# A two-layer graph network on one Trainium2 core: x W0 of the first layer by feature instead of by node

## The reference

```python
def first(x, adj, weight, bias):                 # layer 0
    y = einsum('nm,bmd->bnd', adj, x)
    return einsum('bnd,do->bno', y, weight) + bias

def gru(x, adj, ...):                            # layer 1, 3 steps, in_mat = out_mat = adj
    h = x
    for _ in range(3):
        a = einsum('nm,bmd->bnd', adj, h); av = concatenate([a, a])
        z = sigmoid(lin(av, w3, b3) + lin(h, u3, bu3))
        r = sigmoid(lin(av, w4, b4) + lin(h, u3, bu3))
        hv = tanh(lin(av, w5, b5) + lin(r * h, u5, bu5))
        h = (1 - z) * h + z * hv
    return h

x = layernorm(x + first(x, adj, W0, b0))
x = layernorm(x + gru(x, adj, ...))
```

## Time and profile before

| | us |
|---|---|
| median of 3 runs | 1602.19 (1601.06 to 1602.37) |
| the profiled execution, its time | 1599.25 |
| its span, first to last instruction | 1597.4 |
| TensorE busy | 1583.3 (99%) |
| VectorE busy | 1391.9 (87%) |
| ScalarE busy | 1153.9 (72%) |
| GpSimd busy | 336.0 (21%) |
| DMA | 297.50 MB, mean 186 GB/s |

### The profile page before, as it was taken

One profiled execution on the slowest core, in us unless ns is written; L12 is line 12 of the kernel. 1 busy time (PEld: TensorE's weight loads), 2 busy tenths in 40 slices (PEclk: granted clock), 3 DMA queues, 4 the chain that ended last, 5 costly groups with the idle time before them and its releaser, 6 DMA issues.

```text
span 1597.4 us, 21866 instructions
## 1 busy us (share of the span) xinstructions
PE 1583.3 (99%) x7402; PEld 1327.2 (83%) x7402; DVE 1391.9 (87%) x1416; ACT 1153.9 (72%) x2306; POOL 336.0 (21%) x392
## 2 busy tenths in 40 slices
PE   9999999999999999999999999999999999999996
PEld 8888888888888888888888888888888888888885
DVE  6988888889888898988989898898888898878887
ACT  5677677777777778777777677776777877776666
POOL 5111112123121221212221212212132121110013
PEclk9999999999999999999999999999999999999998
DMA  6555545766467754666646675466755566456544
GB/s 193 173 178 182 191 143 183 222 208 199 144 197 213 222 193 125 202 219 211 198 143 192 222 233 160 161 196 216 219 172 165 188 217 209 141 149 197 170 147 158
DMA packets 215617, 297.50 MB, mean 186 GB/s; under 512 B 21201, under 2 KB 183890, under 8 KB 215506
## 3 DMA queue, kind: packets, MB, share of 16 engines
q1 hardware_dynamic: 215088, 295.79, 59.3%
q10 hardware_dynamic: 418, 0.33, 0.1%
HBM read 149.76 MB, written 146.28 MB: 185 GB/s over the span
## 4 chain that ended last, share of the span: by engine, by line
PE 97%; SPq 1%; ACT 1%; DMA 1%; issue 0%; POOL 0%; DVE 0%; POOLq 0%; ACTq 0%
PE ps_r L462 48%; PE ps_h L462 32%; PE ps_a L562 8%; PE ps_l L519 5%; PE ps_l L529 2%; SPq L321 1%; PE ps_a L543 0%; DMA h_scratch_a<-h_blocks_a 0%; PE ps_a L631 0%; PE ps_l L486 0%; PE ps_h L486 0%; PE ps_l L506 0%; PE ps_h L506 0%; PE ps_a L506 0%; DMA h_landed_a<-h_scratch_a 0%
## 5 line engine op out<-in xcount | busy, mean ns | idle before, releaser
L1068 DVE STREAM_TRANSPOSE a_blocks<-ps_a 128x1024 f32<-128x1024 f32 x92 | 114.8, 1247 | 93.8 <-PE ps_a L562 93.6
L842 ACT ACTIVATE rh<-ps_r,bias_r 128x512 f32<-128x512 f32 x192 | 128.3, 683 | 82.8 <-PE ps_r L462 77.7
L678 ACT ACTIVATE rh_hi<-rh 128x512 fp32r<-128x512 f32 x192 | 119.0, 632 | 75.6 <-DVE rh L1096 75.4
L854 ACT ACTIVATE z_sb<-ps_r,bias_z 128x512 f32<-128x512 f32 x192 | 126.5, 681 | 39.1 <-PE ps_r L462 38.3
L1108 DVE TENSOR_TENSOR hv<-hv,z_sb 128x1024 f32<-128x1024 f32 x95 | 127.6, 1343 | 10.3 <-DVE hv L1105 0.5
L947 DVE TENSOR_TENSOR rh_lo<-rh,rh_hi 128x512 fp32r<-128x512 f32 x192 | 125.7, 688 | 9.2
L858 ACT ACTIVATE hv<-ps_h,bias_h 128x512 f32<-128x512 f32 x192 | 121.0, 676 | 11.9 <-PE ps_h L462 11.9
L462 PE MATMUL ps_r<-a_hi_a,w_hi 128*128 128x512 f32 x384 | 118.8, 391 | 0.5 <-ACT rh L842 0.5
L462 PE MATMUL ps_h<-rh_hi,u_hi 128*128 128x512 f32 x384 | 118.4, 389 | 0.0
L462 PE MATMUL ps_r<-h_hi,u_hi 128*128 128x512 f32 x384 | 118.4, 390 | 0.0
L462 PE MATMUL ps_r<-a_hi_b,w_hi 128*128 128x512 f32 x384 | 118.4, 390 | 0.0
(11 more groups left out here) (395 smaller groups left out, 4295.9 us busy)
## 6 DMA issues: line engine op xcount, KB each, us to landing
h_scratch_a<-h_blocks_a SPq DMA_DIRECT2D x48, 512.0 KB, 5.0
h_landed_a<-h_scratch_a SPq DMA_DIRECT2D x192, 128.0 KB, 2.8
h_scratch_b<-h_blocks_b SPq DMA_DIRECT2D x47, 512.0 KB, 4.2
h_landed_b<-h_scratch_b SPq DMA_DIRECT2D x188, 128.0 KB, 3.1
a_scratch_a<-a_blocks SPq DMA_DIRECT2D x46, 512.0 KB, 2.6
a_landed<-a_scratch_a SPq DMA_DIRECT2D x184, 128.0 KB, 2.9
a_scratch_b<-a_blocks SPq DMA_DIRECT2D x46, 512.0 KB, 2.7
a_landed<-a_scratch_b SPq DMA_DIRECT2D x184, 128.0 KB, 3.0
```

The source lines that it names most:

```text
L678: return act.activation(dst, src, ACT.Copy)
L842: act.activation(rh[:, c, :], ps_r[:, c, :], ACT.Sigmoid, bias=bias_r[:, c:c + 1]).then_inc(r_ready, 1)
L854: act.activation(z_sb[:, c, :], ps_r[:, c, :], ACT.Sigmoid, bias=bias_z[:, c:c + 1]).then_inc(z_ready, 1)
L1068: tr = dve.transpose(flat_blocks(a_blocks).rearrange("p (x e) -> p x e", e=Q), flat(ps_a).rearrange("p (x f) -> p x f", f=Q))
```

## The change

For groups 8 to 31 (`BY_FEATURE`):

- **x W0** has W0's blocks as the stationary operand and x transposed as the moving one: 2 output chunks x 3 parts x 2 input chunks, 12 multiplications of 512 columns. The product stands by feature in `ps_l` and has to be turned back: VectorE transposes it in blocks (`product_blocks`, two operations of 128x512, into `h0_blocks`), SyncE writes it to a new DRAM buffer `xw_scratch` and reads it back into `h_t[g % 8]` in four reads.
- **Slots**: x's transposition goes from 3g-16 to 3g-17 (C to B; group 8 keeps slot 8), and its load from DRAM goes with it (A to C); its write goes a slot earlier (A to C), its reads stay in A (`READ`). The split of the turned x goes from 3g-13 to 3g-14 (C to B), x W0 from 3g-12 to 3g-13 (A to C), with product_blocks (C) and its write and reads in 3g-12 (A). The split of the product (`PARTS`, A), the adjacency product, the sum and the norm stay.
- **Copies**: ScalarE's turned_high and product_high stand behind z's sigmoids instead of ahead of the reset sigmoids, and product_high reads `h_t` and waits for the reads.
- **Layouts**: x's block transposition is written as two operations of half the columns (each chunk's columns in one run), and so is first_sum.
- SyncE in a slot: write of the product, writes of a_blocks, h0 and x, **reads of the product**, reads of an output, of a_blocks, of h0, of x, and the rest as before.

```diff
-    TURN = {g: g - FOUR if g < FOUR + 2 else STEPS * g - 16 for g in LATER}
-    PRODUCT = {g: FIRST_PRODUCTS[g] if g in FIRST_PRODUCTS else STEPS * g - 12 for g in LATER}
+    BY_FEATURE = range(2 * FOUR, GROUPS)
+    TURN = {g: g - FOUR if g < FOUR + 2 else STEPS * g - 16 - (g > 2 * FOUR) for g in LATER}
+    READ = {g: STEPS * g - 15 if g in BY_FEATURE else TURN[g] + 1 for g in LATER}
+    PARTS = {g: FIRST_PRODUCTS[g] if g in FIRST_PRODUCTS else STEPS * g - 12 for g in LATER}
+    PRODUCT = {g: PARTS[g] - (g in BY_FEATURE) for g in LATER}
+    BACK = {g: PRODUCT[g] for g in BY_FEATURE}
...
+                if xw_next is not None:
+                    write_xw(xw_next)
                 if FOUR <= s + 1 < SLOTS:
                     write_a(s + 1)
...
+                if xw_next is not None:
+                    read_xw(xw_next)
                 for g in output_at(s, 1):
                     read_h(nth_move[g, STEPS - 1])
...
+                if g in BY_FEATURE:
+                    for o in range(C):
+                        for n, (v, w) in enumerate(((ax_hi, w0_hi), (ax_hi, w0_lo), (ax_lo, w0_hi))):
+                            for c in range(C):
+                                mm = pe.matmul(ps_l[:, o, :], w[:, c, o * P:(o + 1) * P], v[:, c, :],
+                                               start=n == 0 and c == 0, stop=n == 2 and c == C - 1,
+                                               skip_group_check=True)
...
-                if (g := group_at(s, PRODUCT, -1)) is not None and g > FOUR:
+                if (g := group_at(s, PRODUCT, -1)) is not None and g > FOUR and g not in BY_FEATURE:
                     turned_high(g)
-                if (g := group_at(s, PRODUCT)) is not None:
+                if (g := group_at(s, PRODUCT)) is not None and g not in BY_FEATURE:
                     product_high(g)
...
                     update_gate(s)
+                if (g := group_at(s, PRODUCT, -1)) in BY_FEATURE:
+                    turned_high(g)
+                if (g := group_at(s, PARTS)) in BY_FEATURE:
+                    product_high(g)
...
+            def product_blocks(g):
+                dve.wait_ge(xw_done, g - FOUR + 1)
+                dve.wait_ge(h0_written, 16 * (FOUR + len([k for k in LATER if BLOCKS_AT[k] < BACK[g]])))
+                dve.wait_ge(x_written, 16 * len([k for k in LATER if TURN[k] < BACK[g]]))
+                if g > BY_FEATURE[0]:
+                    dve.wait_ge(xw_written, 16 * (g - BY_FEATURE[0]))
+                for c in range(C):
+                    tr = dve.transpose(h0_blocks[:, :, c * RUN:(c + 1) * RUN].rearrange("p j (b f) -> p j b f", f=Q),
+                                       ps_l[:, c, :].rearrange("p (j b e) -> p j b e", j=BLOCKS, e=Q))
+                tr.then_inc(xw_blocks_ready, 1)
```

More of the change, by code:

```diff
@@ L57, in gnn_kernel @@
     FIRST_PRODUCTS = {FOUR: 2, FOUR + 1: 4, FOUR + 2: 6}
[L58 to L62 removed]
+    BY_FEATURE = range(2 * FOUR, GROUPS)
[4 more added lines that the diff above has]
+    BACK = {g: PRODUCT[g] for g in BY_FEATURE}
+    SUM = {g: PARTS[g] + 1 for g in LATER}
+    MEASURE = {g: PARTS[g] + 2 for g in LATER}
+    NORM = {g: PARTS[g] + 3 for g in LATER}
     BLOCKS_AT = {g: 6 if g == FOUR else NORM[g] for g in LATER}
     def group_at(s, stage, behind=0):
[L67 removed]
+        for g in stage:
             if stage[g] + behind == s:
@@ L388, in read_x, with write_xw, read_xw @@
                 to_quadrants(h_t[g % H_RING][:, :, :, :], x_scratch, x_moved)
+            def write_xw(g):
+                n = g - BY_FEATURE[0]
+                sp.wait_ge(xw_blocks_ready, n + 1)
+                if n >= 1:
+                    sp.wait_ge(xw_moved, n * MOVED)
+                to_dram(xw_scratch, h0_blocks[:, :, :], xw_written)
+            def read_xw(g):
+                sp.wait_ge(xw_written, (g - BY_FEATURE[0] + 1) * 16)
+                to_quadrants(h_t[g % H_RING][:, :, :, :], xw_scratch, xw_moved)
             def store_last():
@@ L433, in _ @@
                     read_h0(h0_next)
-                if x_next is not None:
-                    read_x(x_next)
+                if x_landing is not None:
+                    read_x(x_landing)
                 if h0_next in first_state:
@@ L698, in turned_high @@
                 act.wait_ge(x_moved, (g - FOUR + 1) * MOVED)
+                if g in BY_FEATURE:
+                    copy(in_quadrants(ax_hi), chunks_first(h_t[g % H_RING])).then_inc(xt_hi_ready, 1)
+                    return
                 copy(by_batch_and_chunk(ax_hi).rearrange("p r (j e) -> p j r e", e=Q),
@@ L702, in product_high @@
             def product_high(g):
+                if g in BY_FEATURE:
+                    act.wait_ge(xw_moved, (g - BY_FEATURE[0] + 1) * MOVED)
+                    copy(flat(ax_hi), flat_blocks(h_t[g % H_RING])).then_inc(xw_hi_ready, 1)
+                    return
                 act.wait_ge(xw_done, g - FOUR + 1)
@@ L1002, in turned_low @@
                 dve.wait_ge(xt_hi_ready, g - FOUR + 1)
+                if g in BY_FEATURE:
+                    low_part(in_quadrants(ax_lo), chunks_first(h_t[g % H_RING]), in_quadrants(ax_hi)).then_inc(xt_lo_ready, 1)
+                    return
                 parts = (by_batch_and_chunk(t).rearrange("p r (j e) -> p j r e", e=Q) for t in (ax_lo, ax_hi))
@@ L1009, in product_low @@
                 dve.wait_ge(xw_hi_ready, g - FOUR + 1)
-                low_part(flat(ax_lo), flat(ps_l), flat(ax_hi)).then_inc(xw_lo_ready, 1)
+                low_part(flat(ax_lo), flat_blocks(h_t[g % H_RING]) if g in BY_FEATURE else flat(ps_l),
+                         flat(ax_hi)).then_inc(xw_lo_ready, 1)
+            def product_blocks(g):
[4 more added lines that the diff above has]
+                    dve.wait_ge(xw_written, 16 * (g - BY_FEATURE[0]))
+                for c in range(C):
+                    tr = dve.transpose(h0_blocks[:, :, c * RUN:(c + 1) * RUN].rearrange("p j (b f) -> p j b f", f=Q),
+                                       ps_l[:, c, :].rearrange("p (j b e) -> p j b e", j=BLOCKS, e=Q))
+                tr.then_inc(xw_blocks_ready, 1)
             def first_sum(g):
@@ L1015, in first_sum @@
                 dve.wait_ge(x_biased, g + 1)
+                if g in BY_FEATURE:
+                    by_row = flat(ps_l).rearrange("p (i c b f) -> p c b i f", c=C, b=G, f=Q)
+                    by_batch = rows[:, :, :].rearrange("p b (c i f) -> p c b i f", c=C, f=Q)
+                    for c in range(C):
+                        add = dve.tensor_tensor(by_batch[:, c], by_row[:, c], by_batch[:, c], ALU.add)
+                    add.then_inc(y_added, 1)
+                    return
                 dve.tensor_tensor(rows[:, :, :], by_node(first_banks(g)), rows[:, :, :], ALU.add).then_inc(y_added, 1)
@@ L1027, in first_blocks @@
                     dve.wait_ge(x_written, len(turned) * 16)
+                    if (backs := len([k for k in BACK if BACK[k] < BLOCKS_AT[g]])) >= 1:
+                        dve.wait_ge(xw_written, 16 * backs)
                 if g < FOUR:
@@ L1235, in _ @@
                     low_part(adj_lo[:, :], adjt[:, :], adj_hi[:, :]).then_inc(adj_ready, 1)
-                if (g := group_at(s, PRODUCT)) is not None:
+                if (g := group_at(s, PARTS)) is not None:
                     product_low(g)
+                if (g := group_at(s, BACK)) is not None:
+                    product_blocks(g)
                 if (g := group_at(s, SUM)) is not None:
```

14 lines of the change are left out of this document (12 added, 2 removed).

## The result

The changed kernel takes 1604.25 us (median of 22 runs, 1599.99 to 1607.54) beside 1600.82 of the kernel before in the same runs: ratio 1.0022, interval 1.0016 to 1.0028, so **3.5 us slower** (2.6 to 4.5). Run again later, on two chips, the pair gave 1.0042 (1.0030 to 1.0054) and 1.0014 (1.0005 to 1.0022); whether the chip makes that difference was not tried. The first profiled execution was the slowest of its 22 (1607.54 us, span 1605.7); those of the two later ones took 1607.28 and 1601.73. What I read from one profile I therefore give for all three. Part of an execution's time has nothing to do with the change: the stretch up to slot 3 takes 75.5 to 76.6 us in some profiles and 78.0 to 78.5 in others, whatever the kernel (76.1 in the one of before, 78.2 in the first of after). So profiles are compared by their slots and not by their spans.

A forecast was written before the change was run, and what follows sets the result against it. The prediction took TensorE, busy 99%, to bound the kernel. Its terms, -3.6 + 6.9 + 2.2 = +5.5, took the profiled 1599.25 to 1604.8 us; 2.94 more for the median gave 1607.7, stated as 1607.5, range 1598 to 1614.

The forecast's parts named there:

- The prediction's own signs: Wrong if A is 14.96 us in all forms, or TensorE's waits name a_hi, z's sigmoids or ax_lo.
- The product: x W0 on TensorE: 12 multiplications of 512 columns save 0.15 us a group over 24 groups, -3.6 us.
- rh_hi in A: ScalarE's copies in 12 A slots with two block transpositions miss TensorE's deadline by 0.50 or 0.68 us: +6.9 us.
- rival 2: Only the 12 A slots with two transpositions stall, 3.6 us in all; gain and loss cancel at 1602; chance 0.17.
- rival 1: All hidden in A if GpSimd's addition starts before +2.7 or after the hv operations: 1598.6 us; chance 0.17.
- The sigmoids of A: First reset sigmoid late for a w3 in seven of 24 A slots; bounds 0 and 4.5, taken as 2.2 us.
- turned_low: VectorE's step at B's end, due at 20.2, ends at 18.6 to 20.6: 0 to 0.4 us, taken as nothing.
- SyncE and the DMAs: Transfers, B the tight slot: cover 0.5 us before TensorE waits; taken as 0, up to 3 us kept.
- Rival 3: Product's traffic makes B's graph-product reads late, another 12 to 24 us: 1619 to 1632; chance 0.08.

The follow-up runs named there:

- the bias run: Changed kernel with both halves of GpSimd's bias addition behind the new state: 1607.01 us, 1.0034 of the kernel before.
- turned_low ahead: Changed kernel with the split step turned_low ahead of x's block transposition on VectorE in B, run twice: 1600.06 and 1599.90 us, 1.0001 and 0.9997 of before.
- the run of both: Changed kernel with turned_low ahead of x's transposition and both halves of GpSimd's bias addition behind the state: 1602.01 us, 1.0006 of before.
- no trip: Changed kernel without the product's DRAM write and four reads (output not the reference's), run twice: 1596.22 and 1597.13 us, both 0.9981 of before.
- the form: Kernel before with only x W0 as 12 multiplications of 512 columns, old slots, no transposition back: 1595.61 us, 0.9969 of before.
- the places: Changed kernel with x W0 in its old form, nothing to turn back, all new slots and places kept: 1601.01 us, 1.0011 of before.

## Why the prediction was right, and where it was not

The direction held (forecast +5.5, measured +3.5), but that the size came near is partly luck: one term was more than twice too large, one was put at nothing, and the two errors stood against each other. With C's 5.5 to 9.2 in place of that nothing, the same sum would have been +11 to +15. The prediction's own signs say it too: it called itself wrong if TensorE's waits named z's sigmoids or ax_lo, and ax_lo leads the list (4.2 us, 8 times), with z's sigmoids behind (0.8). In absolute time the forecast of 1607.5 is 3.3 over the measured 1604.25: 2.0 from the sum, and the rest from its baseline, a median of 3 runs (1602.19) where 22 gave 1600.82.

- *The product, -3.6.* Measured alone: 4.3 by the slots, 5.0 by the ratio (3.0 to 6.9). I took 2.87 from the chain's piece; the slot's length, 17.86 against 14.96, already said 2.90.
- *rh_hi in A, +6.9.* The mechanism, the place and the deadline were right: only slots 3 and 6 modulo 12 lose, by what their copies end after 12.30, and the bias run takes it to nothing. The size was not: 2.3 to 2.7, below even the 3.6 of rival 2. I took the delay by GpSimd's addition over from before. VectorE's nat_lo, which ended at 10.9 to 11.5 in these slots, now ends at 10.5 to 10.8, since the addition begins sooner after the slot's start and partly beside a transposition. That was my rival 1, in part: in slot 30 the addition starts at +2.2, ahead of the +2.7 from which I had all hidden, and the slot still loses 0.32.
- *The sigmoids of A, +2.2.* Nothing in any profile of the changed kernel: a w3 begins at 9.52 in every A. It is there with turned_low ahead: one slot and three in its two runs, four in the run of both, 0.55 to 0.6 each. That the squares come later against A once C no longer waits is my reading, not shown.
- *turned_low, "between nothing and 0.4 in the worst slots; I take nothing".* This step failed. Measured: 5.5 to 9.2 us in C. The place was named, with its deadline and the ending range of 18.6 to 20.6 against 20.2; I set it to zero because I let VectorE enter B at 2.8 and a_hi end as before. VectorE entered B at up to 5.3, a_hi began at 14.2 in the mean, not 13.4, and in the slots that cost most at 14.9 to 16.5; turned_low ended at 18.4 to 22.3.
- *SyncE and the DMAs, "I take 0".* This step failed too, and it is the cause of the former. I counted that A gives away as many transfers as it gets and looked at B's queue. But the product's write and reads stand ahead of a_blocks' reads in A, where x's write stood beside and its load behind. Their trip costs 5.3 us (no trip against changed, on one chip).
- *Rival 3* had this mechanism by its other door, in B, at 12 to 24 us and a chance of 0.08: a_blocks' write of B held behind the state's and the output's transfers. In the changed kernel it acts through A and costs about 5; I should have given A's reads a row of their own. Rival 3's own door opens in the run with the product's reads later.

So the account by runs: the form -4.3 to -5.0, the places +1.8 (0.3 to 3.2), the trip about +5. The form and the places add to -3.2 by their ratios, and the run without the trip, on the same chip, gave -3.0: the transposition back costs nothing that can be seen. The Trainium skill, "TensorE: Matmul & The Clock Gate", section "Back-to-back issue gap", would have made the first term an estimated 0.7; the run of the form alone decides against it here.

## What to carry to other kernels

In a kernel bound by one engine at 99%, a saving on that engine of 0.18 us a group is real and measurable; here it was lost again to a trip through memory in front of transfers that were just in time. Before moving a step, list for each queue it passes, the DMA issuer's first, what waits behind it and with how much cover; a balance of bytes per stage doesn't show that. And when a wait removed doesn't shorten the run, look whether the chain that ended last still consists of the bound engine: here it had gone from 97% to 60%, and the busy share of 99% had not moved. And don't trust a mean where a wait begins at a threshold: in the run with the reads later, eight late B slots of 24 made nearly all of the loss in C, under a mean that had hardly moved.

## What was not expected of the hardware

- Multiplications of 512 columns of this type come every 0.2267 us and those of 256 every 0.1196 at a granted clock of 1.00; worked out from the two, the fixed part is 13 ns, and x W0 of 12 x 512 shortened the slot by 0.18 us.
- An addition of GpSimd of 128x512 holds up VectorE's operations with two operands in SBUF (1.90 instead of 1.18 in slot 30), and not its block transpositions (1.25 and 1.20 beside it in the bias run).
- The write of a_blocks, 512 KB, takes 2.9 us from issue to landing in slot 30 without the product's transfers (528.09 to 530.96), 4.5 with the product's write ahead of it (reads later), and 6.0 with the product's four reads behind it as well (529.03 to 534.99).
- 22 executions of the changed kernel spread by 7.5 us (1599.99 to 1607.54), and 22 of the kernel before by 5.3 (1598.87 to 1604.19). Up to 3.0 of either can be the stretch up to slot 3 (75.5 to 78.5 us in the profiles); in the changed kernel the waits of C vary by 3.7 besides.
